# The last layer's attention over positions: maxima subtracted by GpSimd, row sums from extra columns of V, queries copied by ScalarE, and the residual addition inside the next normalisation

## The reference, cut to what matters

```python
ln1 = layer_norm(hidden_states)
qkv = einsum('sbh,oh->sbo', ln1, qkv_weight)     # 16 query heads, 4 groups of keys and values, 8 wide
scores = where(causal, einsum('bgqsd,bgtd->bgqst', qb, kb) * scale, lowest)
attn = softmax(scores, axis=-1)
ao = einsum('bgqst,bgtd->bgqsd', attn, vb)
h1 = hidden_states + einsum('sbh,oh->sbo', ao, proj_weight)
ln2 = layer_norm(h1)                             # then router, experts with a capacity, and
                                                 # h1 + the experts' sum is the block's output
```

## Time and profile before

| what | us |
|---|---|
| median of 3 runs | 3389.8 |
| lowest and highest | 3388.43, 3397.67 |
| the profiled execution: time of the run | 3392.57 |
| the profiled execution: span of the core | 3390.8 |
| busy in it: TensorE / weight loads | 2983.7 / 2221.2 |
| busy in it: VectorE / ScalarE / GpSimd | 2149.1 / 1739.2 / 1280.2 |

### The profile page before, as it was taken

The page is one execution under the profiler, slowest core; times in us unless marked ns, Lnnn a source line. Parts: engine busy times, 40 slices in busy tenths (PEclk is TensorE's granted clock), DMA queues, the critical chain, the costliest instruction groups (busy, mean ns, idle before and its releaser), DMA issues. The chain is left out here.

```text
span 3390.8 us, 67345 instructions
## 1 busy us (share of the span) xinstructions
PE 2983.7 (88%) x21088; PEld 2221.2 (66%) x21088; DVE 2149.1 (63%) x8138; ACT 1739.2 (51%) x4877; POOL 1280.2 (38%) x1455
## 2 busy tenths in 40 slices
PE   6999979969887999999999698999999965675898
PEld 5888734425544788888888456776666754464676
DVE  4544457634555555555555249998999996897332
ACT  5777734422222655555555267777777642232232
POOL 2121247712200333333333037776677765311000
PEclk9999989955598899999999899988999955897899
DMA  3000033210200000000000000000000000001000
GB/s 104 6 5 5 4 76 75 50 53 1 101 6 0 1 0 0 0 0 0 0 0 1 4 6 6 6 5 6 6 7 5 6 29 1 7 13 30 0 0 25
DMA packets 48457, 55.21 MB, mean 16 GB/s; under 512 B 5369, under 2 KB 33545, under 8 KB 47753
## 3 DMA queue, kind: packets, MB, share of 16 engines
q1 hardware_dynamic: 48288, 53.40, 6.1%
HBM read 48.87 MB, written 4.39 MB: 16 GB/s over the span
## 5 line engine op out<-in xcount | busy, mean ns | idle before, releaser
L1610 POOL TENSOR_TENSOR l2a_probs<-l2a_probs,l2a_inv 128x1024 f32<-128x1024 f32 x128 | 242.2, 1892 | 476.8 <-DVE l2a_inv L1776 476.7
L1721 ACT ACTIVATE l2a_probs<-l2a_s_ps,l2a_nm 128x256 f32<-128x256 f32 x512 | 236.7, 474 | 225.9 <-DVE l2a_nm L1752 225.9
L2482 DVE MAX8 l3a_top<-l3a_work 128x8 f32<-128x128 f32 x1536 | 314.3, 277 | 0.0
L2333 PEld LDWEIGHTS l3a_l2o_ps<-net_arena 128*128 128x128 f32 x2048 | 264.0, 212 | 74.0 <-issue 43.1
L2333 PE MATMUL l3a_l2o_ps<-net_arena 128*128 128x128 f32 x2048 | 275.0, 299 | 42.2 <-ACT net_l1f_gate L2389 37.1
L2200 POOL TENSOR_SCALAR l3a_above<-l3a_score,l3a_top 128x128 f32<-128x128 f32 x512 | 298.7, 601 | 17.0 <-DVE l3a_top L2482 6.6
L2484 DVE MATCH_REPLACE8 l3a_work<-l3a_top,l3a_work 128x128 f32<-128x128 f32 x1024 | 269.0, 276 | 0.0
L2323 PE MATMUL l3a_l2h_ps<-net_cols,net_arena 128*128 (+1 forms) x512 | 247.6, 608 | 10.1 <-PEq L1817 7.6
L2317 PEld LDWEIGHTS l3a_o_ps<-l3a_v,l3a_pT 128*128 128x128 f32 x1024 | 154.4, 223 | 119.4 <-ACT l3a_pT L2380 77.4
L681 ACT ACTIVATE l0a_probs<-l0a_score_ps,l0a_nm 128x128 f32<-128x128 f32 x512 | 179.6, 381 | 73.6 <-DVE l0a_nm L730 73.6
L2425 ACT ACTIVATE net_arena<-l3a_l2h_ps,net_l2f_b 128x512 f32<-128x512 f32 x256 | 173.6, 695 | 79.3 <-PE l3a_l2h_ps L2323 78.9
(11 more groups left out here) (528 smaller groups left out, 7239.0 us busy)
## 6 DMA issues: line engine op xcount, KB each, us to landing
l0f_code<-code_rows SPq DMA_DIRECT2D x32, 512.0 KB, 10.5
l0a_c_in<-ctxT SPq DMA_DIRECT2D x32, 64.0 KB, 1.8
net_arena<-L_w1T SPq DMA_DIRECT2D x1, 2048.0 KB
net_arena<-L_w2T SPq DMA_DIRECT2D x1, 2048.0 KB
l3a_k_in<-ctxT SPq DMA_DIRECT2D x32, 64.0 KB, 1.8
l3a_v_raw<-ctx SPq DMA_DIRECT2D x32, 64.0 KB, 2.0
block_out<-l3b_y SPq DMA_DIRECT2D x32, 64.0 KB
l3h_att<-block_out SPq DMA_DIRECT2D x8, 256.0 KB, 4.9
```

The source lines that it names most:

```text
L1610: pool.tensor_tensor(p[:, :, :], p[:, :, :], per_row(inv[c % 2][a][:, :, :].rearrange("p i o -> p (i o)"), KV), ALU.mult).then_inc(scaled, 1)
L1721: act.activation(probs[c % 2][a][:, 2 * i + odd, :], s_ps[a][odd][:, i * KV:(i + 1) * KV], ACT.Exp, bias=nm[c % 2][a][:, i, odd:odd + 1], ...
L2333: ins = pe.matmul(o2_ps[:, j * D:(j + 1) * D], hidden[x][:, i, j * P:(j + 1) * P], w2[:, expert(u, x), i, :], start=(i == 0), stop=(i == C ...
L2482: ins = dve.max(t[:, step // 2, h, :], src)
```

## The change

In `l3_block_attention`: the subtraction of the maxima becomes a GpSimd step `shift` (0) behind `gather` (−1). ScalarE gets a step `take_q` (−1) at the head of its list, which copies the queries; VectorE's `take_k` then waits for that copy and spreads the keys. The V buffers get four more columns for each of the four groups, filled once by GpSimd with the mask of the rows' head, so that `apply` puts the row sums beside the outputs (36 instead of 32 columns for each product); `total` is gone, and `divide` inverts the sums from PSUM. The stage `l3_block_residual` is gone: `normalise` n3m loads `block_out`, adds it to `k.rows` in front of each half's statistics, and adds the gated sum to `k.x` behind the last normalised tile, in front of the copies of the logits.

```diff
+        if attended is not None:
+            att = s.sb("att", [P, NB, D])
+            att_in = [s.sem(f"att_in{g}") for g in range(NG)]
+            joined, x_joined = s.sem("joined"), s.sem("x_joined")
...
+                if attended is not None:
+                    for g in range(NG):
+                        tiles = slice(g * G4, g * G4 + G4)
+                        sp.dma_start(att[:, tiles, :], attended[tiles, :, :].rearrange("b p d -> p b d")).then_inc(att_in[g], 16)
...
                 for half in halves:
+                    if attended is not None:
+                        for g in range(half.start // G4, half.stop // G4):
+                            tiles = slice(g * G4, g * G4 + G4)
+                            dve.wait_ge(att_in[g], 16)
+                            dve.tensor_tensor(k.rows[:, tiles, :], k.rows[:, tiles, :], att[:, tiles, :], ALU.add
+                                              ).then_inc(joined, 1)
+                        dve.wait_ge(joined, half.stop // G4)
                     for t in range(half.start, half.stop):
...
+                if attended is not None:
+                    for g in range(NG):
+                        tiles = slice(g * G4, g * G4 + G4)
+                        dve.scalar_tensor_tensor(out=k.x[:, tiles, :], in0=k.rows[:, tiles, :], scalar=k.tg[:, 7:8],
+                                                 in1=k.x[:, tiles, :], op0=ALU.mult, op1=ALU.add).then_inc(x_joined, 1)
                 if gate_w is not None:
...
-        v = [s.sb(f"v{i}", [P, PJ, P]) for i in range(4)]
+        WV = R * HD + R
+        v = [s.sb(f"v{i}", [P, PJ, GK, WV]) for i in range(4)]
...
                 pool.wait_ge(made, 3 + PJ)
+                for t in v:
+                    pool.tensor_copy(t[:, :, :, R * HD:WV].rearrange("p j g r -> p (j g) r"), per_group(own_head[:, :], PJ * GK)
+                                     ).then_inc(made, 1)
...
-                schedule(pool, [(gather, -1)])
+
+                def shift(q, c):
+                    t = score[c % 2]
+                    wait(pool, maxed, q, 1, c + 1)
+                    pool.tensor_tensor(t[:, :, :], t[:, :, :], per_row(mx[c % 2][:, :], S), ALU.subtract
+                                       ).then_inc(shifted, 1)
+                schedule(pool, [(gather, -1), (shift, 0)])
...
-                            ins = pe.matmul(o_ps[S * j:S * j + S, 32 * g:32 * g + 32], pT[:, g, S * j:S * j + S],
-                                            v[c % 4][:, j, 32 * g:32 * g + 32], start=True, stop=True)
+                            ins = pe.matmul(o_ps[S * j:S * j + S, g, :], pT[:, g, S * j:S * j + S], v[c % 4][:, j, g, :],
+                                            start=True, stop=True)
...
-                schedule(act, [(take_out, 2), (take_p, 1), (exps, 0)])
+
+                def take_q(q, c):
+                    wait(act, k_mm, q, 1, c + 1)
+                    wait(act, s_mm, q, 1, c - 1)
+                    act.activation(qT[c % 2][:, :], q_ps, ACT.Copy).then_inc(q_ready, 1)
+                schedule(act, [(take_q, -1), (take_out, 2), (take_p, 1), (exps, 0)])
...
-                def take_qk(q, c):
-                    wait(dve, k_mm, q, 1, c + 1)
+                def take_k(q, c):
+                    wait(dve, q_ready, q, 1, c + 1)
                     wait(dve, s_mm, q, 1, c - 1)
-                    dve.tensor_copy(qT[c % 2][:, :], q_ps).then_inc(q_ready, 1)
...
-                    wait(dve, maxed, q, 1, c + 1)
-                    dve.tensor_tensor(t[:, :, :], t[:, :, :], per_row(mx[c % 2][:, :], S), ALU.subtract
-                                      ).then_inc(shifted, 1)
-
-                def total(q, c):
-                    wait(dve, exped, q, 1, c + 1)
-                    dve.tensor_reduce(sums[c % 2][:, :], score[c % 2][:, :, :], AX.X, ALU.add).then_inc(summed, 1)
-                    wait(dve, summed, q, 1, c + 1)
-                    dve.reciprocal(inv[c % 2][:, :], sums[c % 2][:, :]).then_inc(inv_ready, 1)
 
                 def divide(q, c):
                     wait(dve, o_mm, q, 1, c + 1)
+                    dve.reciprocal(inv[:, :, :], o_ps[:, :, R * HD:WV]).then_inc(inv_ready, 1)
                     wait(dve, inv_ready, q, 1, c + 1)
...
-                schedule(dve, [(take_qk, -1), (take_v, -1), (soften, 0), (total, 1), (divide, 1)])
+                schedule(dve, [(take_k, -1), (take_v, -1), (soften, 0), (divide, 1)])
```

More of the change, by code:

```diff
@@ L244, in normalise @@
 def normalise(nc, k, name, source="x", twice=False, gain=None, shift=None, keep_rows=False,
-              gate_w=None, columns=None, logits=None, fetch=(), after=None, gains=None):
+              gate_w=None, columns=None, logits=None, fetch=(), after=None, gains=None,
+              attended=None):
     tiled = columns is not None
@@ L2525, in l3_block_attention @@
         score = [s.sb(f"score{i}", [P, H, S]) for i in two]
-        mx, sums, inv = ([s.sb(f"{n}{i}", [P, H]) for i in two] for n in ("mx", "sums", "inv"))
+        mx = [s.sb(f"mx{i}", [P, H]) for i in two]
+        inv = s.sb("inv", [P, GK, R])
         pT = s.sb("pT", [P, GK, P])
@@ L2532, in l3_block_attention @@
         q_ps, k_ps = (qk_ps[:, i * P:(i + 1) * P] for i in range(2))
-        o_ps, aoT_ps, y_ps = (out_ps[:, i * P:(i + 1) * P] for i in range(3))
+        o_ps = out_ps[:, 0:GK * WV].rearrange("p (g w) -> p g w", g=GK)
+        aoT_ps, y_ps = (out_ps[:, GK * WV + i * P:GK * WV + (i + 1) * P] for i in two)
         y_stored = [s.sem(f"y_stored{i}") for i in two]
         (filled, made, staged, k_mm, v_mm, q_ready, k_ready, v_ready, s_mm, s_out, maxed, shifted, exped,
-         summed, inv_ready, p_mm, p_ready, o_mm, ao_ready, aoT_mm, aoT_ready, y_mm, y_ready) = (s.sem(n) for n in (
+         inv_ready, p_mm, p_ready, o_mm, ao_ready, aoT_mm, aoT_ready, y_mm, y_ready) = (s.sem(n) for n in (
              "filled", "made", "staged", "k_mm", "v_mm", "q_ready", "k_ready", "v_ready", "s_mm",
-             "s_out", "maxed", "shifted", "exped", "summed", "inv_ready", "p_mm", "p_ready", "o_mm", "ao_ready",
+             "s_out", "maxed", "shifted", "exped", "inv_ready", "p_mm", "p_ready", "o_mm", "ao_ready",
              "aoT_mm", "aoT_ready", "y_mm", "y_ready"))
@@ L2694, in take_v @@
                     wait(dve, o_mm, q, 1, c - 3)
-                    dve.tensor_tensor(v[c % 4][:, :, :], v_ps[:, :].rearrange("p (j n) -> p j n", j=PJ), own_cols[:, :, :],
-                                      ALU.mult).then_inc(v_ready, 1)
+                    dve.tensor_tensor(v[c % 4][:, :, :, 0:R * HD].rearrange("p j g n -> p (j g) n"),
+                                      v_ps[:, :].rearrange("p (m n) -> p m n", m=PJ * GK),
+                                      own_cols[:, :, :].rearrange("p j (g n) -> p (j g) n", g=GK), ALU.mult).then_inc(v_ready, 1)
                 def soften(q, c):
@@ L2726, in l3_block_residual @@
[L2726 to L2749, removed]
-                    dve.wait_ge(summed, g + 1)
-                    dve.scalar_tensor_tensor(out=k.x[:, tiles, :], in0=k.rows[:, tiles, :], scalar=k.tg[:, 7:8],
-                                             in1=k.x[:, tiles, :], op0=ALU.mult, op1=ALU.add).then_inc(x_done, 1)
@@ L2755, in program @@
+                    dve.tensor_tensor(ao[:, :, :].rearrange("p (g r) d -> p g r d", g=GK),
+                                      o_ps[:, :, 0:R * HD].rearrange("p g (r d) -> p g r d", r=R),
+                                      inv[:, :, :].unsqueeze(3).to_broadcast([P, GK, R, HD]), ALU.mult).then_inc(ao_ready, 1)
+                schedule(dve, [(take_k, -1), (take_v, -1), (soften, 0), (divide, 1)])
 def program(nc, d, out, first=0, last=99):
@@ L2817, in l3_block @@
         l3_block_attention(nc, k)
-        l3_block_residual(nc, k)
-        normalise(nc, k, "n3m", gains=k.l3b_w, source="rows", gain=norms[:, 2:3], shift=norms[:, 3:4],
+        normalise(nc, k, "n3m", attended=k.block_out, gains=k.l3b_w, source="rows", gain=norms[:, 2:3], shift=norms[:, 3:4],
                   gate_w=k.gates_w[:, 3, :], logits=k.logits)
```

5 lines of the change are left out of this document (1 added, 4 removed).

## The result

The changed kernel took 3436.1 us in the median of four runs (3428.8 to 3446.5), the kernel before beside it 3393.7. The ratio is 1.0126, with a 95% interval of 1.0090 to 1.0161: slower. Measured once more, beside later experiments, it was 3429.9 us for 3404.0, a ratio of 1.0088 (1.0061 to 1.0114); the two intervals overlap. The two profiled spans are 3431.0 and, before, 3390.8 us.

What follows compares the result with a forecast made beforehand. TensorE's closed 5.10 us turn bounded the loop, VectorE nearly critical; the change closes a 6.15 us chain through GpSimd. Loop 37.1 + start 1.2 + tail 0.1 − residual 4.4 = +34.0 on 3390.8: 3424 us, range 3405 to 3440.

Steps and rivals of the forecast that it cites:

- The ring: Attention loop: projection(c+1), query copy, K, V, scale, maximum, shift(c), gather(c+2), projection(c+2) form a closed chain; +37.1 us.
- Its length: Attention loop: one turn of that closed chain takes 6.15 us, 5.72 or 6.38 with the ends of the shift.
- the sum: Chain steps in the loop add to 6.15 us a turn; all parts of the change together add +34.0 us.
- P: Attention loop: start of a turn's query projection on TensorE, from which the chain's step times are counted.
- The shift's price: Subtraction of the maxima on GpSimd in the loop: 1.04 us, with ends 0.61 and 1.27.
- Contention: Attention loop: GpSimd could be held up by VectorE; nothing was added for it.
- The clock: Rival: TensorE's clock falls in the loop, turns become 7.7 us, +88 − 3, total 3475 us; 5%.
- Ahead of the loop: GpSimd writes ones columns of four V buffers before its first gather, on the path: 1.2 us, from 0 to 1.6.
- The residual: Last normalisation: only eight additions stay ahead, updates of x hide behind normalised tiles; −4.4 us, between −3 and −5.5.
- TensorE keeping the turn: Rival, attention loop: TensorE's own 5.10 or 5.20 us decides the turn; +2.5 us, total 3392, not slower; 8%.
- VectorE was the bound: Rival, attention loop: VectorE relieved of 1.7 us, turn falls to 4.0 us; −37 us, total 3353, faster; 5%.

Runs made afterwards that it cites:

- second profile: The changed kernel itself, unaltered, run and profiled again beside later experiments: 3429.9 us for 3404.0, ratio 1.0088, loop 209.2 us.
- the reordered loop: Changed kernel with the gather two turns ahead and new step orders on TensorE, ScalarE and VectorE: 3352.8 us for 3397.9, loop 126.5 us.

## Why the prediction was right, and where its sizes were off

I predicted 3424 us, slower at 0.86, in 3405 to 3440; it was 3436.

- *The ring* was the mechanism. Moving the gather, and nothing else, takes 38 of 40.7 us away, and lengthening GpSimd or VectorE beside it does what the ring says: the first is on it, that place of the second is not.
- *Its length* was 6.04 us for the 6.15 of the sum. From P: query copy 0.74 (0.75), K 1.05 (1.09), V 1.66 (1.74), scale 2.26 (2.34), maximum 2.97 (3.06), shift 3.74 (3.83), gather 4.73 (4.87), next projection 6.04. K and V each came 0.03 to 0.04 us sooner after their forerunner than I had put, and the gather 0.05 sooner: it starts 0.99 us behind a shift that lasts 1.05. At the end of each body the turn is 6.21, so the mean without long turns is 6.08: 33 x 0.07 = 2.3 us less than predicted.
- *The shift's price* was taken from the row with the broadcast operand, 1.04; it measured 1.047 in the mean of 24. Against VectorE's 0.69 that is 1.5 times. The Trainium skill, "GPSIMD Engine Reference", 4.1 Engine selection, says about twice; this case doesn't bear that out for float32 with one operand broadcast.
- *Contention* was put at nothing, and the gather's copies last 400 and 613 ns on average in the loop, as before (403, 613). By the Trainium skill, "SBUF — State Buffer", Who interferes with whom, a VectorE tensor_tensor contends with GpSimd's reads when both its inputs lie in SBUF, and a reduction never does. These copies, beside VectorE operations with at most one tensor input in SBUF, agree.
- *The clock* was the term that was mis-sized. I had it as a rival for the whole loop, 7.7 us a turn, all or nothing, gave the sum nothing for it, and named a clock below its upper level in the loop as a sign of being wrong. It came in part: four turns of 7.1 to 8.0 us, together 5.9 us above 6.08 each, six turns and 8.2 us in the second profile. The price of a whole turn at the lower level was near, 8.09 us for 7.7; I had counted 0.69 us of waiting for ScalarE, and it is 1.06, since TensorE also waits 0.37 ahead of the output projection. That only some turns would be slow was not on my list. The range held because its upper end had been set by other doubts, those on the shift's price, and that is luck.
- *Ahead of the loop*: the four column copies took 0.77 us together and put the first gather back by 0.7, but the first scale by only 0.4 us; I took 1.2.
- *The residual*: −4.4 us predicted, 304.5 − 308.8 = −4.3 measured from the last scale to the end (−5.1 where it was done alone), the parts as read: four additions, loads landing late (1.85 us wait for the second pair), the updates of x under the normalised tiles.
- *The total*: 203.0 − 2.3 + 5.9 = 206.6 for the loop; with 0.4 at the start and −4.3 at the end the changed stretches cost 36.8 us where the sum had 34.0. That it came so near is partly luck: the ring (2.3 us) and the start (0.8) were put too long, the clock 5.9 too low. Of the 12 us between 3424 and 3436 these are some 3. Another 4 are the kernel before, 3393.7 beside the changed one for the 3389.8 that I had added to; the rest, 5 to 6, lies outside the changed stretches, as do 3.4 us of the 40.2 between the two spans.
- *The range* of the forecast stands twice, as 3408 to 3438 and as 3409 to 3433; only the second follows from the turn's 5.72 to 6.38.
- *The rivals*: TensorE keeping the turn needed the gather to be free, and where it was made free the result was its 3392 (3393.4 measured). That VectorE was the bound, 3353, was false for this kernel, yet 3352.8 is what came when the orders were changed with it. That agreement is partly chance: it was worked out as TensorE's busy share, and TensorE's share is the bound there.

## What to carry to other kernels

Before giving an idle in-order engine more work, ask what stands behind it in that engine's queue and whether what it waits for depends, a turn or two on, on that very thing; if so, the prefetch must be issued further ahead, which cost two lines here and returned 38 us. Work taken off the engine with the highest busy share is worth nothing while a ring of hand-overs closes the turn, and was worth 30 us here once the order inside the turn let TensorE run at 94% and VectorE at 87%. Where the part of a program ahead of the change varies by 30 us, measure the stretch that is changed.

## What the runs showed of the hardware

A loop in which TensorE waits 0.85 us a turn, and is busy 13 to 14 of 20 us, lost its full clock (1.00) at one or two places behind its cold start, at 1 to 3 us each, though its waits behind the start were no longer than 1.02 us; with three matmuls more a turn it kept it. And in the reordered loop GpSimd's shift of 1.047 us ran beside 17 us in 20 of VectorE work without getting longer (1047 ns in the mean of 18).
